# Rows of a graph layer spread over the partitions by two small DMAs through a table in DRAM, not by matmuls on TensorE; the first term's dots taken first

## The reference

```python
deg = segment_sum(ones, col)
dis = clip(deg, 1.0) ** (-0.5)
norm = dis[row] * dis[col]
gnn = x1                                   # xn @ W1 + b1
for k in range(4):
    Wi, Wj = (Wg[k, :h], Wg[k, h:])
    alpha = tanh(gnn[col] @ Wi + gnn[row] @ Wj + bg[k])
    agg = segment_sum(norm[:, None] * alpha * gnn[row], col)
    gnn = gnn + agg
```

## Time and profile before

| | |
|---|---|
| median of three runs | 750.36 us |
| profiled execution, its own time | 751.38 us |
| its span | 749.6 us, clock 0.998 |
| TensorE busy | 725.4 us, 97%, 3833 instructions |
| DVE busy | 546.0 us, 73% |
| ACT busy | 400.0 us, 53% |
| POOL busy | 200.0 us, 27% |
| DMA | 109.08 MB, mean 146 GB/s |
| chain that ended last | PE 45%, of it L2014 26%, L1861 4%, L1869 1% |

### The profile page before, as it was taken

How to read it: one execution, slowest core, us unless ns; L and a number is a source line. 1 busy time by engine, 2 the same in 40 slices (tenths; PEclk the granted TensorE clock), 3 DMA queues, 4 the chain that set the end, 5 groups by cost and what they waited for, 6 DMA issues and landing times. The chain is left out here.

```text
span 749.6 us, 10598 instructions
## 1 busy us (share of the span) xinstructions
PE 725.4 (97%) x3833; PEld 648.8 (87%) x3836; DVE 546.0 (73%) x1057; ACT 400.0 (53%) x818; POOL 200.0 (27%) x202
## 2 busy tenths in 40 slices
PE   5999999999999999998998999999999999999998
PEld 4999888999998999977766888888888889998886
DVE  6898885654559999877678788898966767674331
ACT  5534343644648888758575475764753342563220
POOL 5358888874204641112022200000020020000000
PEclk9999999999999999999999999999999999999999
DMA  6977555546444553699453592342252463244331
GB/s 239 322 195 182 118 141 128 122 90 224 121 130 110 134 130 89 227 279 269 140 114 113 147 259 85 114 151 69 91 127 85 126 137 138 85 158 148 117 126 43
DMA packets 39684, 109.08 MB, mean 146 GB/s; under 512 B 12552, under 2 KB 13624, under 8 KB 39248
## 3 DMA queue, kind: packets, MB, share of 16 engines
q1 hardware_dynamic: 25360, 89.83, 36.2%
q0 software_dynamic: 13920, 16.38, 13.9%
q10 hardware_dynamic: 352, 2.20, 0.8%
HBM read 96.31 MB, written 2.83 MB: 132 GB/s over the span
## 5 line engine op out<-in xcount | busy, mean ns | idle before, releaser
L1306 DVE TENSOR_TENSOR w_lo<-raw,w_hi 128x1024 fp32r<-128x1024 f32 x140 | 170.0, 1222 | 71.5 <-ACT w_hi L995 71.0
L995 ACT ACTIVATE w_hi<-raw 128x1024 fp32r<-128x1024 f32 x140 | 147.6, 1058 | 103.7 <-PE bank L2014 80.5
L1962 PE MATMUL bank<-xn1T,w_hi 128*128 128x384 f32 x416 | 106.0, 335 | 0.0
L2014 PE MATMUL bank<-w_hi,xn3T 128*128 128x512 f32 x288 | 92.3, 393 | 0.0
L844 POOL DMA_INDIRECT count_table<-total,place x48 | 83.8, 1746 | 25.7 <-issue 14.0
L1962 PEld LDWEIGHTS bank<-xn1T,w_hi 128*128 128x128 f32 x416 | 74.8, 188 | 0.1
L1962 PE MATMUL bank<-xn1T,w_lo 128*128 128x384 f32 x208 | 69.5, 334 | 0.0
L2014 PEld LDWEIGHTS bank<-w_hi,xn3T 128*128 128x128 f32 x288 | 54.1, 188 | 11.0
L844 POOL DMA_INDIRECT mask_table<-value,place x48 | 53.4, 1112 | 31.0 <-issue 12.8
L1962 PE MATMUL bank<-xn4T,w_hi 128*128 128x384 f32 x240 | 61.1, 335 | 0.0
L2014 PE MATMUL bank<-w_lo,xn3T 128*128 128x512 f32 x144 | 56.0, 389 | 0.0
(11 more groups left out here) (356 smaller groups left out, 1684.5 us busy)
## 6 DMA issues: line engine op xcount, KB each, us to landing
raw<-weights SPq DMA_DIRECT2D x140, 512.0 KB, 3.6
row_sb<-rows SPq DMA_DIRECT2D x6, 512.0 KB, 6.0
kcat<-kcat POOLq DMA_DIRECT2D x16, 192.0 KB, 3.7
base<-rows POOLq DMA_DIRECT2D x6, 512.0 KB, 13.0
w1r<-w_in ACTq DMA_DIRECT2D x1, 2048.0 KB, 8.4
w2r<-w_in SPq DMA_DIRECT2D x1, 2048.0 KB, 11.2
row_sb<-rows SPq DMA_DIRECT2D x6, 256.0 KB, 5.0
base<-x_in SPq DMA_DIRECT2D x1, 1536.0 KB, 7.0
```

The costliest lines, as they stand in the source:

```text
L995: act.activation(w_hi[:, u % RING], raw[:, u % RAW], ACT.Copy).then_inc(hi_split, 1)
L1306: dve.tensor_tensor(w_lo[:, u % RING], raw[:, u % RAW], f(w_hi[:, u % RING]), ALU.subtract).then_inc(unit_split, 1)
L1962: last = pe.matmul(out_of(pr)[:, 0:N], w[pa][:, slot, k * P:(k + 1) * P], TT[src][:, pb, k], start=(k == 0 and m == 0), stop=(k == KD - 1 ...
L2014: last = pe.matmul(out_of(pr)[:], tile[:, pa, k, ts], w[pb][:, at_, j * HALF:(j + 1) * HALF], start=(kk == 0 and j == 0 and m == 0 and nam ...
```

## The change

The row is now spread by DMA. POOL gets a step `row_out`, directly behind `hop_dot` (and for dis behind `g1_out` 0): it waits for the column, writes it to a table of 384 words in DRAM (`row_table[n]`, element by element, node order), waits until that has landed, and reads the table back into all 128 partitions (`ai_row` or `dis_row`, 128 x 384). ACT's tanh waits for that landing in place of the bank. The five spreads, their banks and their waits go from TensorE. DVE takes the three dots of the first term (`j` = 0) first and raises `row_dotted` behind the third, so that POOL can begin while the other three are taken.

```diff
-    after = {1: [("hop_dot", 0)], 2: [("norm",)], 3: [("hop_row", 0), ("hop_mul", 0)], 4: [("hop_msg", 0), *exps("q", 0, 0)],
...
-             11: [("hop_sum", 1), ("queries", 1), *ends("k", 0, 2)], 12: [("hop_dot", 2)],
-             14: [("context", 0), ("hop_row", 2), ("hop_mul", 2)], 15: [("hop_msg", 2), ("y", 0, 0)],
...
+             10: [("queries", 0), *exps("k", 0, 2), *ends("k", 0, 1)], 11: [("queries", 1), *ends("k", 0, 2)],
+             14: [("context", 0)], 15: [("y", 0, 0)], 16: [("y", 0, 2), *exps("q", 1, 0)],
...
+    for h, (dot, row, msg, total) in enumerate(((1, 3, 4, 6), (6, 8, 9, 11), (12, 14, 15, 16), (17, 19, 20, 22))):
+        for at_, own in ((dot, [("hop_dot", h), ("row_out", h)]), (row, [("hop_row", h), ("hop_mul", h)]), (msg, [("hop_msg", h)]),
+                         (total, [("hop_sum", h)])):
+            here = after.setdefault(at_, [])
+            if own[0][0] in ("hop_sum", "hop_dot"):
+                here.extend(own)
+            else:
+                here[0:0] = own
...
+                if s[0] == "row_out":
+                    n = s[1]
+                    if n < HOPS:
+                        pool.wait_ge(row_dotted, n + 1)
+                    else:
+                        pool.wait_ge(dis_ready, 1)
+                    pool.dma_start(row_table[n].rearrange("(t p) o -> p (t o)", p=P),
+                                   aij[:, 0] if n < HOPS else dis[:, 1], allow_slow_non_contiguous=True).then_inc(row_stored[n], 16)
+                    pool.wait_ge(row_stored[n], 16)
+                    if n < HOPS:
+                        if n:
+                            pool.wait_ge(tanh_done, n)
+                        pool.dma_start(ai_row[:], row_table[n].rearrange("n o -> (n o)").partition_broadcast(P)).then_inc(ai_landed, 16)
+                    else:
+                        pool.dma_start(dis_row[:], row_table[n].rearrange("n o -> (n o)").partition_broadcast(P)).then_inc(dis_landed, 16)
...
-                    wait_full(act, f"ai.{n}")
+                    act.wait_ge(ai_landed, 16 * (n + 1))
...
-                        ins = act.activation(msg[:, t], out_of(f"ai.{n}")[:, 0:N], ACT.Tanh, bias=aij[:, 1, t:t + 1])
-                    emptied(ins, f"ai.{n}")
+                        ins = act.activation(msg[:, t], ai_row[:], ACT.Tanh, bias=aij[:, 1, t:t + 1])
+                    ins.then_inc(tanh_done, 1)
...
-                    for t in range(NT):
-                        for j in range(2):
...
+                    for j in range(2):
+                        for t in range(NT):
...
+                            if (j, t) == (0, NT - 1):
+                                ins.then_inc(row_dotted, 1)
...
-                if kind == "hop_row":
-                    n = s[1]
-                    pe.wait_ge(aij_ready, n + 1)
-                    spread(f"ai.{n}", lambda t: aij[:, 0, t:t + 1])
```

More of the change, by code:

```diff
@@ L182, in schedule @@
                   ("xn3_lo", 1), tiled("g1", 0, 1, 0, 2), ("x_norm", 2), ("xn3_T", 2), tiled("g1", 0, 1, 2, 4),
-                  ("xn3_hi", 2), ("xn3_lo", 2), ("g1_out", 0), tiled("g1", 0, 2, 0, 2), tiled("g1", 0, 2, 2, 4),
+                  ("xn3_hi", 2), ("xn3_lo", 2), ("g1_out", 0), ("row_out", HOPS), tiled("g1", 0, 2, 0, 2), tiled("g1", 0, 2, 2, 4),
                   ("g1_out", 1), ("ahead",), ("ahead",), ("g1_out", 2)])
@@ L190, in ends @@
         return [("soft_end", name, c, t) for t in tiles]
-    after = {1: [("hop_dot", 0)], 2: [("norm",)], 3: [("hop_row", 0), ("hop_mul", 0)], 4: [("hop_msg", 0), *exps("q", 0, 0)],
[L193 to L196, removed]
-             11: [("hop_sum", 1), ("queries", 1), *ends("k", 0, 2)], 12: [("hop_dot", 2)],
-             14: [("context", 0), ("hop_row", 2), ("hop_mul", 2)], 15: [("hop_msg", 2), ("y", 0, 0)],
[L199 to L203, removed]
-             23: [("queries", 3), *ends("k", 1, 2)]}
@@ new lines, in schedule @@
+    after = {2: [("norm",)], 4: [*exps("q", 0, 0)],
+             5: [*exps("q", 0, 1), *ends("q", 0, 0)], 6: [*exps("q", 0, 2), *ends("q", 0, 1)],
+             7: ends("q", 0, 2), 8: [*exps("k", 0, 0)], 9: [*exps("k", 0, 1), *ends("k", 0, 0)],
+             10: [("queries", 0), *exps("k", 0, 2), *ends("k", 0, 1)], 11: [("queries", 1), *ends("k", 0, 2)],
+             14: [("context", 0)], 15: [("y", 0, 0)], 16: [("y", 0, 2), *exps("q", 1, 0)],
+             17: [*exps("q", 1, 1), *ends("q", 1, 0), ("transpose_y", 0)],
+             18: [*exps("q", 1, 2), *ends("q", 1, 1)], 19: [("transpose_y", 1), *ends("q", 1, 2)], 20: [*exps("k", 1, 0)],
+             21: [("queries", 2), *exps("k", 1, 1), *ends("k", 1, 0)], 22: [*exps("k", 1, 2), *ends("k", 1, 1)],
+             23: [("queries", 3), *ends("k", 1, 2)]}
@@ L360, in plan_banks @@
             product("degree", 0)
-        elif kind == "norm":
-            product("norm", 7)
         elif kind == "mix0_kT":
@@ L395, in plan_banks @@
                 product(f"xn3.{s[1]}.{b}", 6 + b)
-        elif kind == "hop_row":
-            product(f"ai.{s[1]}", 3 * (group % 2) + 2)
         elif kind == "hop_sum":
@@ L521, in gps_kernel @@
         gjunk = at("gjunk", [P, 2, HID], F32, MASK)
+        ai_row = at("ai_row", [P, N], F32, AT + 27)
+        dis_row = at("dis_row", [P, N], F32, AT + 28.5)
         k2n = at("k2n", [P, 2, NT, HALF], F32R, R3)
@@ L591, in tiles_of @@
             return tab[0:N * N].rearrange("(t p m) o -> p t (m o)", p=P, m=N)
+        row_table = [nc.dram_tensor(f"row_table{n}", (N, 1), F32, kind="Internal").ap() for n in range(HOPS + 1)]
         key_table = nc.dram_tensor("key_table", (EC, P), F32, kind="Internal").ap()
@@ L643, in gps_kernel @@
         g_ready = sem("g_ready")
+        row_stored, ai_landed, dis_landed = [sem(f"row_stored{n}") for n in range(HOPS + 1)], sem("ai_landed"), sem("dis_landed")
+        tanh_done, normed, row_dotted = sem("tanh_done"), sem("normed"), sem("row_dotted")
         base3_ready, base4_ready = sem("base3_ready"), sem("base4_ready")
@@ L1490, in _ @@
                 if kind == "norm":
-                    wait_full(dve, "norm")
+                    dve.wait_ge(dis_landed, 16)
                     for t in range(NT):
-                        ins = dve.scalar_tensor_tensor(count[:, t], count[:, t], dis[:, 1, t:t + 1], out_of("norm")[:, 0:N],
+                        ins = dve.scalar_tensor_tensor(count[:, t], count[:, t], dis[:, 1, t:t + 1], dis_row[:],
                                                        ALU.mult, ALU.mult)
                         if t == NT - 1:
-                            emptied(ins, "norm")
+                            ins.then_inc(normed, 1)
                         else:
@@ L1732, in _ @@
                     wait_row(dve, f"wg{n}")
-                    for t in range(NT):
-                        for j in range(2):
[L1735 to L1738, removed]
+                    if n:
+                        dve.wait_ge(row_stored[n - 1], 16)
+                    for j in range(2):
+                        for t in range(NT):
+                            if (j, t) == (1, 1):
+                                dve.wait_ge(row_dotted, n + 1)
+                            dve.wait_ge(v_chain, vn[0] - (t + j > 0 and (j, t) != (1, 0)))
+                            ins = dve.tensor_tensor_reduce(out=gjunk[:, (j + t) % 2], in0=g[:, t],
+                                                           in1=row(f"wg{n}", j * HID, (j + 1) * HID),
+                                                           scale=1.0, scalar=0.0, op0=ALU.mult, op1=ALU.add,
+                                                           accum_out=aij[:, j, t:t + 1])
+                            if (j, t) == (0, NT - 1):
+                                ins.then_inc(row_dotted, 1)
+                            else:
+                                note(ins)
                     noted()
@@ L1742, in _ @@
                     if s[1] == 0:
-                        wait_emptied(dve, "norm")
+                        dve.wait_ge(normed, 1)
                         noted()
-                    wait_emptied(dve, f"ai.{s[1]}")
+                    dve.wait_ge(tanh_done, s[1] + 1)
                     dve.tensor_tensor(msg[:], msg[:], count[:], ALU.mult).then_inc(msg_f, 1)
@@ L1870, in transposes @@
                 full(last, name)
[L1872 to L1878, removed]
             pe.wait_ge(consts, 2)
@@ L1917, in _ @@
                         full(last, "degree")
-                if kind == "norm":
-                    pe.wait_ge(dis_ready, 1)
-                    spread("norm", lambda t: dis[:, 1, t:t + 1])
                 if kind in ("unit", "part", "first_k"):
```

## The result

The changed kernel takes **803.02 us** (median of five, 801.18 to 804.06) against 750.36 us before: a ratio of 1.0687, with a 95% interval of 1.0669 to 1.0704. It is 52.7 us slower. I had forecast 749.7, with 754.0 as the high end.

What follows compares the result with a forecast made beforehand. TensorE, busy 20.00 of 20.00 us, was taken as the bound: -3.3 for spreads, +1.7 and +0.8 of waits at hops 1 and 2, about -0.7 us, so 750.36 became 749.7; range 748.1 to 754.0.

Steps and rivals of the forecast that it cites:

- What goes: Five spreads leave TensorE's busy path, for dis and hops 0 to 3: 3.3 us saved.
- T: Way through DRAM from the third dot's end to the start of tanh, in four steps: 5.9 us.
- The column goes to the table: Second step of T, the store of 384 elements to DRAM: 2.4 us, from a scatter of 128 elements.
- upper bound of 4.4: Store step of T if the 0.96 us issue grew with the elements: 0.96 x 3 + 1.47 = 4.4 us.
- The read: Third step of T, the row coming back to 128 partitions, 192 KB: 3.1 us.
- ACT's wake: Last step of T, before tanh starts: 0.1 us, an estimate.
- the worst landing: T of 14 us, with 192 KB transfers on the same queue landing after 9.5 us at most.
- The frame of the sum: Spreads saved against TensorE stalls per hop that grow with T: -3.3 + 1.7 + 0.8 = about -0.7 us.
- The places for hops 0 to 2: hop_sum 0 no stall up to T = 6.0; transposes of queries 1 stall 1.7 us; y stalls 0.8 us.
- Hop 3: TensorE arrives at hop_sum 3 at 544.6, msg's low half ends at 543.8: no stall up to T = 6.7.
- For the norm row nothing waits: Its two DMAs hang on dis, ready before the last tiles of g1, far ahead of count's scaling: no wait.
- The rival on the slower side: Store's issue grows by the element: T = 7.9, +6.3 us, 756.7; it decides from T = 6.65; chance 0.28.

Runs made afterwards that it cites:

- the run with cover: Against the kernel with runs of 12 bytes: row, mul and msg of every hop, and hop_sum 2, one unit later; 758.50 us, ratio 1.0089.
- the two sets of stores: Kernel before plus eight probe DMAs per set on POOL after hop_sum 0, varying word count, spacing and piece size; 384 packed words landed after 10.3 us.
- runs of 12 bytes: Changed kernel with each partition's three words side by side in the table and tanh reading with a stride; 771.06 us, ratio 1.0258.
- the run with words: Kernel before with only the norm row spread by two DMAs, stored as 4-byte words, hop rows still by matmuls; 753.01 us, ratio 1.0023.

## Why the prediction was wrong

- **What goes** was right: the five spreads are gone, and TensorE's busy time, where the clock hardly falls, goes down by about what they cost (the run with cover: 722.6 against 725.4).
- **The step that failed** is the second of T: "The column goes to the table", taken at 2.4 us from the scatter of 128 words. It measured 10.1, and 7.7 of the 10.3 us by which T was too short lie there. The scatter's words go to places all over a table of 576 KB; those of the row lie side by side, and that, not their number, is the price, as the two sets of stores show. I had looked for a row with the same size of piece, where it took one with the same places. My upper bound of 4.4 multiplied the issue by three, which was the wrong part: the issue is 0.8.
- **The read**, taken at 3.1, measured 5.2 to 6.5. By itself it is 3.7. With ACT's wake this step has the other 2.6 us. T came to 16.2 instead of 5.9; I had written that by the worst landing T is 14, and had left it out of the range.
- **The frame of the sum held.** Its own rule at T = 16.2 gives 10.2 for hop 0, 12.0 for hop 1, 11.1 for hop 2 and 9.5 for hop 3, 42.8 in all; measured are 14.0, 12.9, 10.2 and 7.3, 44.4. With runs of 12 bytes, at T = 8.7, it gives 2.7, 4.5, 3.6 and 2.0, 12.8 in all; measured are 3.4, 4.8, 2.5 and 2.5, 13.2. That the sums come so close is in part luck, since hops 0 and 3 miss to opposite sides at the long T. The places for hops 0 to 2 were right: hop_sum 0, the transposes of queries 1, y. Hop 3 waits ahead of the transposes of queries 2, one unit before hop_sum 3; the prediction had not looked at them. Hop 0 is longer because its dots start at 432.34 instead of 429.50.
- **"For the norm row nothing waits"** was wrong in its reach: nobody waits for the row, but the store of dis holds the weights, and that makes the dots late (2.7 us of wait in the run with words).
- **A term was missing:** the clock. 12.2 us are paid by matmuls at 1.2 GHz behind the four waits. I put nothing for it and counted a wait of TensorE as its own length.
- **The rival on the slower side** had the sign and the wrong mechanism: the issue grows by some 0.2 us for three times the pieces, not threefold (0.76 to 0.80 us for 384 words, 0.54 to 0.57 for 128 runs). The rule of the Trainium skill that stood beside it ("DMA: Bandwidth & Descriptors", section "Rules for kernel authors") says one descriptor per element, and to make the last dimension contiguous instead. The count of descriptors is not the price here, for the 384 words 512 bytes apart are as many and land in 2.1 us; the advice is borne out, for runs of 12 bytes land in 2.3 to 2.7 in the kernel. The same page's section "Anatomy of one DMA — SWDGE (gpsimd) path" puts most of a DMA's fixed time into the receipt of the write, above all in HBM; the trace agrees in kind, for at hop 0 all data packets have started by 436.2 and the completions come from 440.8 to 444.3, but not in size.

## What to carry to other kernels

In this case a small store was priced by where its pieces land: before single words are put side by side in DRAM, make runs of 12 bytes of them, and let the reader take the stride. A way through DRAM is free only where the engines that wait for it have other work for its whole length. And a wait of TensorE can cost, beside its own length, the slower matmuls after it: here a wait of 3.39 us (runs of 12 bytes, hop 0) made the 27 matmuls take 8.98 us, nearly as long as the 9.09 behind a wait of 14.0.

## What the hardware showed that I had not expected

- 128 or 384 words of 4 bytes, packed in DRAM, land after 8.2 to 10.3 us; the same words 512 bytes apart after 2.1.
- Such a store holds other queues: at hop 0 the sixteen 4 KB packets of weights that start from 438.5 to 438.8, within it, take 2.5 to 7.8 us, by the trace's packets, where the median is 0.16.
- Behind a wait of 14.0 us TensorE's clock is at 0.50, and 27 matmuls take 9.09 us; kept busy through the same wait, it stays at 1.00, and they take 6.38.
